# Second stage of a two-stage linear layer: two nested levels of seven products in place of one, sums of blocks on GpSimd, the residual in the weights

## The reference

```python
def _L0_cond_ref(x, weight, bias, lora_a_weights, lora_b_weights, scaling_factors, adapter_id):
    base = jnp.einsum('bsi,oi->bso', x, weight) + bias
    low = jnp.einsum('bsi,bri->bsr', x, lora_a_weights[adapter_id])        # rank 16, an adapter per batch
    delta = jnp.einsum('bsr,bor->bso', low, lora_b_weights[adapter_id])
    return base + scaling_factors[adapter_id][:, None, None] * delta

def _L0_ffn_ref(x, codes, absmax, bias):
    w = _dequant_nf4(codes, absmax)                                        # 4-bit codes, blocks of 64
    return jnp.einsum('bsd,od->bso', x, w) + bias

x = x + _L0_ffn_ref(_L0_cond_ref(x, ...), L0_ffn_codes, L0_ffn_absmax, L0_ffn_bias)
```

## Time and profile before

| | |
|---|---|
| median of three runs | 2213.1 us |
| span of the profiled execution | 2211.8 us (the page gives no time of its own beside the span) |
| TensorE busy | 2166.8 us, 98% of the span |
| VectorE busy | 1790.3 us, 81% |
| ScalarE busy | 1016.5 us, 46% |
| GpSimd busy | 46.8 us, 2% |
| DMA, mean | 252 GB/s |

### The profile page before, as it was taken

The page is one execution under the profiler, slowest core; times in us unless marked ns, Lnnn a source line. Parts: engine busy times, 40 slices in busy tenths (PEclk is TensorE's granted clock), DMA queues, the critical chain, the costliest instruction groups (busy, mean ns, idle before and its releaser), DMA issues.

```text
span 2211.8 us, 31548 instructions
## 1 busy us (share of the span) xinstructions
PE 2166.8 (98%) x12104; PEld 1859.8 (84%) x12104; DVE 1790.3 (81%) x2647; ACT 1016.5 (46%) x1277; POOL 46.8 (2%) x55
## 2 busy tenths in 40 slices
PE   4899999999999999999999999999999999999999
PEld 4688788788878778899999988888988889888888
DVE  8899889768974664688778898888898887988887
ACT  8655555555553333444444443343443434443432
POOL 5100000000000000000000000000000000000000
PEclk8999999999999999999999999999999999999999
DMA  9688788887887897777777887777977877877775
GB/s 285 218 255 268 226 260 267 261 257 240 271 260 237 276 306 228 270 239 239 234 244 233 271 283 240 241 245 246 304 251 240 253 245 257 289 249 246 239 244 173
DMA packets 381172, 558.00 MB, mean 252 GB/s; under 512 B 23376, under 2 KB 234992, under 8 KB 380896
## 3 DMA queue, kind: packets, MB, share of 16 engines
q1 hardware_dynamic: 377712, 544.95, 77.6%
q0 software_dynamic: 3312, 11.03, 1.6%
HBM read 427.96 MB, written 128.99 MB: 252 GB/s over the span
## 4 chain that ended last, share of the span: by engine, by line
PE 91%; DVE 4%; DMA 3%; issue 1%; ACT 0%; SPq 0%; DVEq 0%; ACTq 0%
PE ps L1441 26%; PE ps L1273 14%; PE ps L1275 14%; PE ps L1274 14%; PE ps L1442 13%; PE ps L1445 4%; PE ps L1288 2%; PE ps L1444 2%; DMA rq<-xc_d 1%; PE ps L1321 1%; PE ps L1269 1%; DMA xc_d<-rq 1%; DMA xr<-xc_d 0%; DVE low_tw L966 0%; DVE tile L987 0%
## 5 line engine op out<-in xcount | busy, mean ns | idle before, releaser
L1441 PE MATMUL ps<-comb,xs 128*128 128x512 f32 x2527 | 903.3, 395 | 0.8 <-DVE comb L1047 0.8
L767 ACT CAST xs<-xr 128x1024 fp32r<-128x1024 f32 x427 | 448.3, 1051 | 629.8 <-DMA xr<-xc_d 628.9
L1442 PE MATMUL ps<-comb,xs 128*128 128x256 f32 x2527 | 707.8, 280 | 0.0
L1053 DVE TENSOR_TENSOR xs<-xr,xs 128x1024 fp32r<-128x1024 f32 x427 | 521.4, 1221 | 130.8 <-ACT xs L767 127.8
L1441 PEld LDWEIGHTS ps<-comb,xs 128*128 128x128 f32 x2527 | 474.3, 188 | 103.5 <-DVE comb L1047 1.1
L1442 PEld LDWEIGHTS ps<-comb,xs 128*128 128x128 f32 x2527 | 475.4, 188 | 14.5
L1273 PE MATMUL ps<-wq,tile 128*128 128x512 f32 x1088 | 468.2, 430 | 1.9 <-DVE tile L987 1.8
L1275 PE MATMUL ps<-wq,tile 128*128 128x512 f32 x1088 | 427.5, 393 | 0.0
L1274 PE MATMUL ps<-wq,tile 128*128 128x512 f32 x1088 | 426.1, 392 | 0.0
L1273 PEld LDWEIGHTS ps<-wq,tile 128*128 128x128 f32 x1088 | 205.2, 189 | 70.1 <-ACT cs L735 3.5
L1275 PEld LDWEIGHTS ps<-wq,tile 128*128 128x128 f32 x1088 | 204.9, 188 | 45.0
(11 more groups left out here) (119 smaller groups left out, 2219.8 us busy)
## 6 DMA issues: line engine op xcount, KB each, us to landing
xr<-xc_d SPq DMA_DIRECT2D x427, 512.0 KB, 4.0
raw<-in_L_cond_weight_dram SPq DMA_DIRECT2D x128, 512.0 KB, 4.8
xc_d<-rq SPq DMA_DIRECT2D x26, 1792.0 KB, 7.5
res<-in_x_dram SPq DMA_DIRECT2D x64, 512.0 KB, 5.2
out_dram<-res SPq DMA_DIRECT2D x128, 256.0 KB, 4.5
wc_d<-cs SPq DMA_DIRECT2D x32, 896.0 KB, 4.6
comb_raw<-wc_d SPq DMA_DIRECT2D x28, 1024.0 KB, 7.8
x_nat<-in_x_dram SPq DMA_DIRECT2D x104, 256.0 KB, 3.9
```

Source lines behind the costliest of these rows:

```text
L767: nc.scalar.copy(xs[f][:, HI, :, :], xr[f][:, LO, :, :]).then_inc(s_xhi, 1)
L1053: tt(xs[f][:, LO, :, :], xr[f][:, LO, :, :], xs[f][:, HI, :, :].bitcast(F32), ALU.subtract).then_inc(s_xlo, 1)
L1441: nc.tensor.matmul(bank[:, :], x_hi, both, start=(k == 0), stop=False)
L1442: nc.tensor.matmul(bank[:, 0:HW], x_lo, high, start=False, stop=False)
```

## The change

The first stage stays, except that 16 matmuls of 128 columns add the identity to the diagonal tiles of the combined matrix (line 1635 of the new kernel), so that no rows of x are loaded as a residual.

In the second stage the seven products are nested. The outer level has seven combinations i (`OUTER`); for each, the eight batches q of 512 rows, which gives 56 units u. A unit is an inner level of seven products k (`INNER`): 128 rows by 512 columns with 4 steps of contraction. Products 0, 2, 4 and 6 add up in one PSUM bank (or one pair of banks), 1 and 3 in another, and the state of the bank is added to a result `r_sb` after each product, so that a product starts only when the one before it in the bank has been added or copied (`evacuated`). In units 0 to 31 the products other than 1 and 3 are written in two column halves of 256 and 256 or 272.

The inner sums of x are made by GpSimd (`sum_x`, four of 128 x 512 for each unit), and so are the inner sums of the weights (`sum_blocks`, two groups of four of 128 x 1024 for each i), which go to DRAM (`wi_d`) and come back. Results are carried between outer combinations through DRAM (`m_d`), 1 MB stored and 1 MB loaded a unit. In units 48 to 55 the last combination finishes two outputs of 1 MB: VectorE's `add_last` makes one, GpSimd's the other, and two MB are loaded and stored. At the last batch of an i the seven weight matrices of the next, 1 MB each, are loaded, rounded and split in halves; this happens six times. The x of a unit is loaded as two blocks into one buffer `xg`, which is free again once all seven splits of the unit before are done.

```diff
@@ -100,9 +96,27 @@
...
+    OUTER = [A11, S2, S4, S3, A12, A22, SS1]
+    BASE_OF = {1: 0, 2: 1, 3: 1, 4: 0, 5: 3}
+    FINAL = 4
+    LAST = NF - 1
+    INNER = [A11, SS1, S2, S4, S3, A12, A22]
+    QB = NB
+    NU = NF * QB
+    LOWS = FINAL * QB
...
+    HALF = QT // 2
+    CW = SW + R
+    WITH_LOW = [A11, S2, S3, A12]
...
+    LO_STEPS = {2: [0], 3: [1], 4: [2, 3], 5: [4], 6: [5, 6], 7: [7], 8: [8, 9], 9: [10], 10: [11, 12], 11: [13]}
...
+    def lo_halves(u, k):
+        i, q = divmod(u, QB)
+        if q == QB - 1 and i < LAST:
+            return [(i + 1, n) for n in LO_STEPS.get(k, [])]
+        if q == 0 and i:
+            return [(i, n) for n in LO_STEPS.get(NF + k, [])]
+        return []
...
+            def load_x(u):
+                i, q = divmod(u, QB)
+                for t in range(2):
+                    sp.dma_start(xg[:, t, :, :, :].rearrange("p h k t -> p (h k) t"), xc_d[2 * q + t, OUTER[i]]
+                                 ).then_inc(s_xg, 16)
...
+            def load_total(u, m):
+                q = u % QB
+                if u > BOTH:
+                    sp.wait_ge(s_out[m], 32 * (u - BOTH))
...
+                for t in range(2):
+                    sp.dma_start(total[m][:, t, :, :].rearrange("p n o -> p (n o)"), m_d[2 + m, q, :, t, :]
+                                 ).then_inc(s_tld[m], 16)
...
+            def store_total(u, m):
+                sp.wait_ge(s_fin[m], u - BOTH + 1)
+                for t in range(2):
+                    sp.dma_start(out_block(u % QB, t, m, 1), total[m][:, t, :, :].rearrange("p n (c o) -> p (n c) o", c=2)
+                                 ).then_inc(s_out[m], 16)
...
+            for u in range(NU):
+                i, q = divmod(u, QB)
+                turn = q == QB - 1 and i < LAST
+                if 1 <= u <= BOTH:
+                    store_sums(u - 1, 1)
+                if u > BOTH:
+                    for m in range(2):
+                        store_total(u - 1, m)
+                if u + 1 < NU:
+                    sp.wait_ge(s_xlo, NF * (u + 1))
+                    load_x(u + 1)
+                if u + 1 < LOWS:
...
+                for k in range(NF):
+                    if turn:
+                        sp.wait_ge(s_prod, NF * u + k + 1)
+                        for c in range(2):
+                            load_half_comb(i + 1, INNER[k], c)
+                    if k == 1 and QB <= u + 1 < BOTH:
+                        load_base(u + 1)
...
+                    if k == 1 and u >= BOTH:
+                        for m in range(2):
+                            load_total(u, m)
...
+            def sum_blocks(i, c):
...
+                tt(b11, b12, b11, ALU.subtract).then_inc(s_ws, 1)
...
+                tt(b12, b22, b12, ALU.subtract).then_inc(s_ws, 1)
...
+                tt(b22, b22, b11, ALU.subtract).then_inc(s_ws, 1)
...
+                tt(b21, b21, b22, ALU.subtract).then_inc(s_ws, 1)
...
+            def sum_x(u, steps):
...
+                for n in steps:
+                    if u:
+                        pool.wait_ge(s_prod, NF * (u - 1) + n + 2)
...
+            def add_last(u):
+                pool.wait_ge(s_add, added(u, 5))
+                pool.wait_ge(s_cpy, copied(u, 6))
+                pool.wait_ge(s_lev, 4 * (u - BOTH + 1))
+                tt(total[1][:, :, :, :], total[1][:, :, :, :], r_sb[u % 2][:, :, :, :], ALU.add).then_inc(s_fin[1], 1)
...
+            for u in range(NU):
+                i, q = divmod(u, QB)
+                if u + 1 < NU:
+                    sum_x(u + 1, range(4))
+                if i < LAST and q in (2, 4):
+                    sum_blocks(i + 1, q // 2 - 1)
+                if u >= BOTH:
+                    add_last(u)
...
+            def comb_lo(i, n):
+                f, c = halves_of(i)[n]
+                ks = slice(HALF * c, HALF * (c + 1))
+                dve.wait_ge(s_chi, 2 * NF * i + n + 1)
+                tt(cw[f][:, ks, LO, 0:SW], cr[f][:, ks, LO, 0:SW], cw[f][:, ks, HI, 0:SW].bitcast(F32),
                    ALU.subtract).then_inc(s_clo, 1)
...
+            def add_last(u):
+                dve.wait_ge(s_add, added(u, 5))
+                dve.wait_ge(s_cpy, copied(u, 6))
+                dve.wait_ge(s_lev, 4 * (u - BOTH) + 2)
+                tt(total[0][:, :, :, :], total[0][:, :, :, :], r_sb[u % 2][:, :, :, :], ALU.add).then_inc(s_fin[0], 1)
...
+                    if not fresh(u) or k not in COPIED:
+                        add_product(u, k)
+                    if k == 4 and LOWS <= u < BOTH:
+                        add_lora(u)
+                    if u >= BOTH and k == 5:
+                        add_lora_pair(u, 0)
+                        add_lora_pair(u, 1)
+                    if u >= BOTH and k == 6:
+                        add_last(u)
+                        add_lora_pair(u, 2)
+                        add_lora_pair(u, 3)
...
+                    if u + 1 < NU:
+                        for f in {3: (A11, SS1), 4: (S2,), 5: (S4, S3), 6: (A12, A22)}.get(k, ()):
+                            x_lo(u + 1, f)
+                    for n, h in lo_halves(u, k):
+                        comb_lo(n, h)
...
+                    if k == 0 and s and TILE_ORDER[s - 1] // OT == j:
+                        pe.wait_ge(s_ident, 1)
+                        col = TILE_ORDER[s - 1] % OT * P
+                        nc.tensor.matmul(acc[g % 2][:, col:col + P], ident_r[:, :], ident_r[:, :],
+                                         start=False, stop=False)
...
+            def multiply(u, k):
+                i, q = divmod(u, QB)
+                f = INNER[k]
+                if q == 0:
+                    pe.wait_ge(s_clo, max(half_at(i, f, c) for c in range(2)))
...
+                pe.wait_ge(s_xlo, NF * u + k + 1)
+                if k == 0 and u >= 2:
+                    evacuated(u - 2, 6)
...
+                if k in (2, 3, 4, 6):
+                    evacuated(u, {2: 0, 3: 1, 4: 2, 6: 4}[k])
...
+                for kt in range(QT):
+                    x_hi, x_lo = xs[f][:, HI, kt, :], xs[f][:, LO, kt, :]
+                    w_hi, w_lo = cw[f][:, kt, HI, :], cw[f][:, kt, LO, :]
+                    first, last = opens and kt == 0, kt == QT - 1
+                    if not split:
+                        ins = three(big[:, bank, :], x_hi, x_lo, w_hi[:, 0:SW], w_lo[:, 0:SW], first, last and not lora,
+                                    not opens)
+                        continue
+                    for n, (x, w) in enumerate(((x_hi, w_hi), (x_hi, w_lo), (x_lo, w_hi))):
+                        begin, end = first and n == 0, last and n == 2
+                        nc.tensor.matmul(big[:, bank, 0:HW], x, w[:, 0:HW], start=begin, stop=end,
+                                         skip_group_check=not opens)
+                        ins = nc.tensor.matmul(big[:, bank + 1, 0:wide], x, w[:, HW:HW + wide], start=begin, stop=end,
+                                               skip_group_check=not opens)
...
+            for u in range(NU):
+                for k in range(NF):
+                    multiply(u, k)
+                    if 2 * QB < u <= LOWS and k == 1:
+                        transpose_low(2 * (u - 2 * QB) - 1)
+                    if 2 * QB <= u < LOWS and k == 5:
+                        transpose_low(2 * (u - 2 * QB))
+                    if LOWS <= u < BOTH and k == 3:
+                        multiply_lora(u)
+                    if u >= BOTH:
+                        for n in {3: (0,), 4: (1,), 6: (2, 3)}.get(k, ()):
+                            multiply_lora_pair(u, n)
```

More of the change, by code:

```diff
@@ L196, in wide_before, with fresh, adds_of, added @@
-    def wide_before(i):
-        return sum(is_wide(n) for n in range(i))
+    def fresh(u):
+        return u < QB or u >= BOTH
+    def adds_of(u):
+        return 3 if fresh(u) else 8 if u >= LOWS else 7
+    def added(u, k):
+        before = sum(adds_of(n) for n in range(u))
+        if fresh(u):
+            return before + k - 2
+        return before + k + 1 + (1 if u >= LOWS and k > 4 else 0)
+    def copied(u, k):
+        return 4 * (u if u < QB else QB + u - BOTH) + COPIED.index(k) + 1
@@ new lines, in halves_of, with half_at, half_bytes @@
+    def halves_of(i):
+        if i:
+            return [(f, c) for f in INNER for c in range(2)]
+        return [(A11, 0), (A11, 1), (SS1, 0), (SS1, 1), (S2, 0), (S4, 0), (S2, 1), (S4, 1),
+                (S3, 0), (S3, 1), (A12, 0), (A12, 1), (A22, 0), (A22, 1)]
+    def half_at(i, f, c):
+        return 2 * NF * i + halves_of(i).index((f, c)) + 1
+    def half_bytes(i, f, c):
+        if f not in DIRECT:
+            return 16 * (i + 1)
+        return 32 * (i + 1) + (16 if (f, c) == (S4, 1) else 0)
@@ L623, in _ @@
+            for m in range(2):
+                store_total(NU - 1, m)
+            for n in range(2):
+                sp.wait_ge(s_rst[n], 32 * (BOTH // 2))
+                sp.wait_ge(s_out[n], 32 * QB)
         @block.gpsimd
```

1020 lines of the change are left out of this document (578 added, 442 removed).

## The result

The changed kernel takes 2298.05 us (median of 4 runs, 2293.04 to 2302.87), the kernel before 2213.35 beside it: a ratio of 1.0384, 95% interval 1.0367 to 1.0401. It is slower by 3.8%, 115 us above the forecast, above its range and above the 2245 of the range for 8 in 10. The profiled execution took 2300.26 us.

The account below looks back on a forecast made before the run. The prediction took TensorE's matmuls to bound the kernel: 2032.5 us without stalls, plus start 30, turns 48, weight sums 18, last units 38 and end 15, gave 2181.5 of span, forecast 2183 us, range 2130 to 2206 (8 in 10: 2085 to 2245).

Parts of the forecast that it names:

- The price of the block sums: Units beside GpSimd's inner weight sums: VectorE held up, +1.5 us twelve times, 18 us.
- that row: Profile row of the old kernel: VectorE's `L966` takes 1.21 us alone, 4.42 overlapping GpSimd's 2.37 us sum.
- rival 2: GpSimd and VectorE exclude each other at every meeting: block sums 5 us each, turns 14, total 2272; chance with above 0.15.
- rival 3: TensorE's clock falls behind about 20 new gaps, 1.5 us each, 30 us: 2213; chance with sums near it 0.13.
- The term of 36 us: Block sums priced by the skill's exclusion rule instead of 18 us; with turns at 11 to 12 each, 38 us more.
- The turns: Six weight reloads between outer combinations: VectorE falls behind and x lands late, +8 us each, 48 us.
- The last eight units: Units 48 to 55: late x and output sums make units 26.7 us against 20.85 of matmuls, +38 us.
- The start: Start of the second stage: inner weight sums, stores and loads delay the first products, +30 us, bounds 20 and 40.
- The matmuls: TensorE's second-stage work after the change: 1131 us, 177 less than the 1308 before.
- 20.1: Calm part of the second stage: units taking more than 20.1 us would show the prediction wrong.
- Rival 4: Matmuls in groups of 12 come at 0.235 instead of 0.2267 us, adding 30 us; counted inside the range.
- Rival 1: Stalls mostly hidden: start 20, turns 3 each, no block sums, last units 15, end 13: 2100 us; chance 0.24.

Follow-up runs that it names:

- 1: Changed kernel with nearly all arithmetic of the inner weight sums left out after the first index, all transfers and waits kept: 2238.93 us.
- 3: Changed kernel with each GpSimd weight-sum subtraction of 128x1024 made as four of 128x256: 2241.85 us.
- 5: Changed kernel with weight sums in parts of 256 columns, plus adapter columns loaded two units ahead into two buffers: 2213.01 us.
- 11: Kernel with all four edits (2183 us), plus seven unused 512 KB DRAM copies in each of the six turns: 2220.73 us.
- 12: Kernel with all four edits (2183 us), plus seven unused VectorE subtractions of 128x1024 in each of the six turns: 2220.5 us.
- 6: Changed kernel with weight sums in parts, plus x loaded before the totals' stores in the last eight units: 2233.65 us.
- 7: Weight sums in parts and x loaded before the totals' stores, plus both last-unit sums of 128x2048 on VectorE: 2220.16 us.
- 10: Kernel with all four edits (2183.24 us), plus the four x sums of each unit moved from GpSimd to VectorE: 2186.54 us.

## Why the prediction was wrong

**The price of the block sums** is the step that failed most. 18 us were predicted, 71.8 measured, and 59 go when the arithmetic goes (1). The prediction said: "3 us; 0 if that row is a chance. I take half." The row was no chance: its `L966` ends at 56.85, 1.1 us behind the GpSimd sum, near its own 1.21, as a split of 0.69 us here ends 0.54 behind its sum. The twelve units lose 59.0 us, 4.9 each, which is the 5 of rival 2. Of this some 41 us are waiting, 3.4 a unit: the 3 us that the prediction had and then halved. The other 18 are products at half clock, 1.5 a unit, which the sum left to rival 3. The last 12.8 of the 71.8, in units 12, 20 and 28, the sum did not have at all. They stay for the most part without the arithmetic (10.4 in 1, 13.1 in 3) and go when `a_br` is loaded earlier (1.1 in 5). The rule of the Trainium skill ("SBUF — State Buffer", section Who interferes with whom) is borne out: instructions with two SBUF inputs wait (1637 ns against 681), additions with one input in PSUM don't (684 against 685), for the length of an instruction (3). The term of 36 us that the prediction worked out by it is 23 short of the 59.

**The turns**: 8 each predicted, bounds 5 to 14, measured 13.8. VectorE's queue and the late loads were named rightly, and the size is at its upper bound. What was missing is the wait for `a_br` in VectorE's queue, 5.97 us in unit 8: the sum counted a's columns as small work and not as a load that comes last on a full queue, and the sum put half clock at nothing (some 15 us of the 82.9). Loading it earlier gives back 11.8 us in the turns and 29 in all (5). That both DMA and VectorE count was said, and 11 and 12 bear it out. The gaps stand before products 2, 4 or 5, and 6, released by VectorE.

**The last eight units**: 38 predicted, bounds 15 to 50, measured 51.8. The chain was right, with the gap in front of product 6; the length of 26.7 us was in fact 28.5 to 30.9. The two splits beside GpSimd's sum take 5.70 instead of 1.28 us, and the product behind the gap comes at half clock (some 12 us in all). Loading x earlier gives 9 us of the excess and moving that sum off GpSimd 12 (6, 7).

**The start**: 30 predicted, bounds 20 to 40, measured 38.7: idle gaps of 9.63, 9.69, 3.98 and 9.85 us. The last is in part `a_br` again (5 us go in 5). It is inside the bounds. The matmuls (1135.8 against 1131) and the end (15.9 against 15) are close. Calm units take 19.93, 20.19 and 20.36 us where 20.08 and 19.95 were expected; the last two are above the 20.1 that the prediction named as a sign of being wrong, which costs 5 us. Rival 4's 30 us did not come. VectorE is busy 1613.5 us and not "about as now" (1790.3), GpSimd 548.0 and not 490: its 512-column sums take 1.28 to 1.5 us where 1.2 was estimated, its four block sums 10.8 and not 9.5.

**The rivals.** Rival 2 comes nearest: its terms 30, 84, 60, 50 and 16 against 38.7, 82.9, 71.8, 51.8 and 15.9, with the matmuls 26 us short in all; it had a chance of 0.15. For the block sums its cause is the right one. For the turns its 84 is luck: it has them from GpSimd and VectorE excluding each other, but taking the x sums off GpSimd gives the turns only 5 us (10), while loading `a_br` earlier gives 11.8 (5). Rival 3's mechanism came true beside it, not in its place: some 56 us of slow products where 30 were expected, in a granted clock of 0.94 over the second stage. The prediction counted exclusion and clock each on top of its own sum and never together. Rival 1 fell: the starts, turns and last units were all felt by TensorE.

## What to carry to other kernels

An engine that is busy 24% of the time can still set the time, if it locks out one that others wait for: price work on GpSimd by the VectorE instructions with two SBUF inputs that it will meet, once for each GpSimd instruction, and cut GpSimd's instructions to about the length of VectorE's (here a loss of 59 us became 3) or give the work to VectorE. In a queue that works in order, ask of each instruction not how long it takes but which load it waits for, and what stands behind it: a difference of 64 columns held back the addition that product 4 waited for. And when stalls of some 3 us and more are expected, add a half-clock product behind most of them to the price.
